# Banded attention between two feed-forward stages: rows transposed block by block, rotary products joined, work regrouped on four engines

## What is computed

```python
# hidden = layernorm(x); 16 heads of 64; b, s, _ = hidden.shape
q = rope(hidden @ Wq.T + bq)          # by head: x * cos + rot(x) * sin
k = rope(hidden @ Wk.T + bk)
v = hidden @ Wv.T + bv
# blocks of W = 128 positions; block n sees keys of blocks n - 1 and n
scores = einsum('bhnqd,bhnkd->bhnqk', qb, kcat) / sqrt(64)
band = (kj >= qi) & (kj <= qi + W)    # block 0 of a batch sees only its own keys
attn = softmax(where(valid, scores, -1e30))
ctx = einsum('bhnqk,bhnkd->bhnqd', attn, vcat)
x = x + merged(ctx) @ Wo.T + bo
```

## Time and profile before

| what | value |
|---|---|
| timed runs (3) | median 1627.08 us, 1626.82 to 1629.59 |
| the profiled execution's own time | 1629.63 us |
| its span, first to last instruction | 1627.8 us |
| TensorE busy, matrix products | 1503.2 us (92%) |
| VectorE busy | 1403.6 us (86%) |
| ScalarE busy | 1324.8 us (81%) |
| GpSimd busy | 1137.7 us (70%) |
| mean granted TensorE clock | 0.979 of full speed |

### The profile page before, as it was taken

One profiled execution on the slowest core, in us unless ns is written; L12 is line 12 of the kernel. 1 busy time (PEld: TensorE's weight loads), 2 busy tenths in 40 slices (PEclk: granted clock), 3 DMA queues, 4 the chain that ended last, 5 costly groups with the idle time before them and its releaser, 6 DMA issues. The chain is left out here.

```text
span 1627.8 us, 46830 instructions
## 1 busy us (share of the span) xinstructions
PE 1503.2 (92%) x16866; PEld 1145.2 (70%) x16866; DVE 1403.6 (86%) x3859; ACT 1324.8 (81%) x2442; POOL 1137.7 (70%) x911
## 2 busy tenths in 40 slices
PE   5999878899999999999999999999999999869998
PEld 4888745576767676666767676767676767658887
DVE  5999668899989999999999898999898889857885
ACT  5999658888878888888888787888788878749996
...
GB/s 210 92 124 99 65 100 128 169 164 176 169 183 159 176 161 184 165 187 170 170 184 157 172 166 169 168 176 172 173 151 175 165 166 159 172 157 69 109 111 70
DMA packets 728445, 247.92 MB, mean 152 GB/s; under 512 B 688148, under 2 KB 715032, under 8 KB 728216
## 3 DMA queue, kind: packets, MB, share of 16 engines
...
q10 hardware_dynamic: 704, 0.40, 0.1%
...
## 5 line engine op out<-in xcount | busy, mean ns | idle before, releaser
L1283 DVE CUSTOM_DVE_ANT_0 at_prob<-banks,at_masks,pre_s_scale 128x256 f32<-128x256 f32 (+1 forms) x1024 | 421.3, 472 | 25.8 <-PE banks L1697 9.3
L1446 ACT ACTIVATE at_prob<-at_prob,at_top 128x256 f32<-128x256 f32 (+1 forms) x1024 | 428.3, 490 | 16.5 <-DVE at_top L1283 14.1
L1295 DVE TENSOR_TENSOR at_halves<-at_prob,at_halves 128x1024 f16<-128x1024 f32 (+1 forms) x256 | 331.7, 1296 | 3.1 <-ACT at_halves L1455 3.1
L1582 PE MATMUL banks<-at_xt,pre_w_h 128*128 128x512 f16 x1024 | 299.4, 385 | 12.4 <-ACT at_v_l L1474 7.6
L1697 PE MATMUL banks<-at_kt,at_qt 32*128 32x256 f32 (+1 forms) x4096 | 253.4, 384 | 31.5 <-issue 20.8
L1455 ACT ACTIVATE at_halves<-at_prob 128x1024 f16<-128x1024 f32 (+1 forms) x256 | 263.4, 1029 | 6.1
L1697 PEld LDWEIGHTS banks<-at_kt,at_qt 32*128 32x128 f32 x4096 | 198.6, 187 | 93.1 <-issue 88.4
L1653 PE MATMUL banks<-at_v_h,at_pt 128*128 128x65 f16 x1984 | 208.9, 195 | 32.7 <-DMA at_pt<-at_halves 25.8
L1653 PEld LDWEIGHTS banks<-at_v_h,at_pt 128*128 128x128 f16 x1984 | 182.1, 98 | 73.2 <-DMA at_pt<-at_halves 41.0
L1175 POOL TENSOR_TENSOR at_kt<-at_k_by 128x512 f32<-128x512 f32 x128 | 171.5, 1340 | 77.3 <-DVE at_halves L1295 65.6
L1165 POOL TENSOR_TENSOR at_q_by<-at_q_first,at_tables 128x512 f32<-128x512 f32 x128 | 175.5, 1375 | 61.5 <-DVE at_halves L1295 60.8
...
## 6 DMA issues: line engine op xcount, KB each, us to landing
...
```

What stands on the lines that cost most here:

```text
L1283: last = nc.vector.tensor_tensor_reduce(out=prob[:, n % 2, h, low:2 * P], in0=s_ps[:, h, n % 2 * 2 * P + low:(n % 2 + 1) * 2 * P], in1=mas ...
L1295: nc.vector.tensor_tensor(parts[:, 1, :, :], prob[:, n % 2, :, keys_from(t, b):2 * P], parts[:, 0, :, :], ALU.subtract).then_inc(p_low, 1)
L1446: last = nc.scalar.activation(at, at, ACT.Exp, bias=top[:, n % 2, h:h + 1], scale=-1.0)
L1582: last = nc.tensor.matmul(pr_ps[:, half, :].rearrange("p (b t) -> p b t", b=SB), w[wp][:, k, at:at + P], xt[:, r, xp, :, k, :], start=n == ...
```

## The change

It has five parts, all in the attention stage.

- `x_halves` and `xt` are laid out by block, and `turn_x` transposes one block at a time, in SyncE's turn t block t + 7, behind the probabilities of block 2. Only the first group is still turned at once (`first_turn_x`). The load and the store of residual rows move behind it, and the load comes one turn earlier.
- The cosines and the sines of a group are loaded in different turns (`load_table`).
- GpSimd's turn has another order: the output bias comes first, the key rotation early, `context_low` last and for step t - 1 instead of t - 2, and the last query rotation waits for one more low half.
- VectorE makes its two products in one operation: the bank is read twice by a broadcast, the sine and cosine places are read as one piece (`key_products`, `query_products`), and the four semaphores of products become three.
- ScalarE's low half of the second pair of value blocks comes after two of the four exponentials of block 3 instead of after all four.

The core of the diff; the query's functions change as the key's do, and the indices of `x_halves` and `xt` where they are used follow the new layout:

```diff
-    x_halves = sb("x_halves", [P, 2, SB, C], F16)
-    xt = sb("xt", [P, 2, 2, SB, CK, P], F16)
+    x_halves = sb("x_halves", [P, SB, 2, C], F16)
+    xt = sb("xt", [P, 2, SB, 2, CK, P], F16)
...
-    k_made = [sem(f"k_product{n}") for n in range(4)]
-    q_made = [sem(f"q_product{n}") for n in range(4)]
+    k_first_made = [sem("k_first_by_cos"), sem("k_first_by_sin")]
+    q_first_made = [sem("q_first_by_cos"), sem("q_first_by_sin")]
+    k_second_made = sem("k_second_made")
+    q_second_made = sem("q_second_made")
...
+    def xt_turned(n):
+
+        S, blk = divmod(n, SB)
+        return 16 * (SB * (S // 2) + blk + 1) if S % 2 else 16 * (1 + SB * (S // 2 - 1) + blk + 1) if S else 16
+
     def xt_ready(S):
 
-        return 16 * (S // 2 + 1)
+        return xt_turned(SB * S + SB - 1)
...
-        def turn_x(S):
-
-            if big(S):
-                sp.wait_ge(x_low, SB * (S + 1))
+        def first_turn_x():
+            sp.wait_ge(x_low, SB)
+            sp.wait_ge(past.moved[0], past.stores(2 * past.SLOTS))
+            sp.dma_start(xt[:, 0, :, :, :, :].rearrange("p b e k t -> p (b e k) t"),
+                         x_halves[:, :, :, :].rearrange("p b e c -> p (b e c)"),
+                         transpose=True).then_inc(xt_in[0], 16)
+
+        def turn_x(n):
+
+            if step(n):
+                S, blk = divmod(n, SB)
+                sp.wait_ge(x_low, n + 1)
+                sp.wait_ge(xt_in[(n - 1) // SB % 2], xt_turned(n - 1))
                 need(v_done[1], NG * (S - 1))
-                if S < 2:
-                    sp.wait_ge(past.moved[S], past.stores(S + 2 * past.SLOTS))
-                sp.dma_start(xt[:, S % 2, :, :, :, :].rearrange("p e b k t -> p (e b k) t"),
-                             x_halves[:, :, :, :].rearrange("p e b c -> p (e b c)"),
+                if n == SB:
+                    sp.wait_ge(past.moved[1], past.stores(1 + 2 * past.SLOTS))
+                sp.dma_start(xt[:, S % 2, blk, :, :, :].rearrange("p e k t -> p (e k) t"),
+                             x_halves[:, blk, :, :].rearrange("p e c -> p (e c)"),
                              transpose=True).then_inc(xt_in[S % 2], 16)
...
-        def load_tables(S):
+        def load_table(S, e):
 
             if big(S):
-                for n in range(4):
-                    need(q_made[n], NG * (S - 1))
-                    need(k_made[n], NG * (S - 1))
+                for products in (*q_first_made, *k_first_made, q_second_made, k_second_made):
+                    need(products, NG * (S - 1))
                 at = SB * P * (S % SPB)
-                for e, table in enumerate((cos, sin)):
-                    sp.dma_start(tables[:, S % 2, e, :], table[:, at:at + SB * P]).then_inc(tab_in[S % 2], 16)
+                sp.dma_start(tables[:, S % 2, e, :], (cos, sin)[e][:, at:at + SB * P]).then_inc(tab_in[S % 2], 16)
...
             turn_p(t - 1, 3)
-            if g == 0:
-                turn_x(S + 1)
+            if t == -4:
+                first_turn_x()
             turn_context(t - 2)
             turn_p(t, 0)
-            load_residual(t - 4)
-            store(t - 6)
-            if g == 0 and S >= 0:
-                load_tables(S + 1)
             turn_p(t, 1)
             turn_p(t, 2)
+            if t + 7 >= SB:
+                turn_x(t + 7)
+            load_residual(t - 3)
+            store(t - 6)
             if t == -8:
                 load_x(SB)
             load_x(t + 13)
+            if g == 3 and S >= -1:
+                load_table(S + 2, 0)
+            if g == 1 and S >= 0:
+                load_table(S + 1, 1)
...
         def key(t, half):
 
             if step(t):
-                pool.wait_ge(k_made[2 * half], t + 1)
-                pool.wait_ge(k_made[2 * half + 1], t + 1)
+                pool.wait_ge(k_first_made[half], t + 1)
+                pool.wait_ge(k_second_made, t + 1)
                 need(s_done, 2 * t - 2)
                 need(k_carried, carried(t - 2))
                 nc.gpsimd.tensor_tensor(kt[:, half, own(t, 0):own(t, 0) + SB, :].rearrange("p s t -> p (s t)"),
-                                        k_by[:, 2 * half, :], k_by[:, 2 * half + 1, :],
+                                        k_by[:, half, :], k_by[:, 3 - half, :],
                                         (ALU.subtract, ALU.add)[half]).then_inc(k_roped[half], 1)
...
-            context_low(t - 2)
+            if t <= STEPS:
+                bias_rows(t - 5)
+            if t >= STEPS:
+                bias_rows(t - 4)
             key_product(t + 1, 0)
-            key_product(t + 1, 3)
+            key_product(t + 1, 1)
+            key(t + 1, 1)
             after_p_low(t, 0)
-            key(t + 1, 1)
+            key(t + 1, 0)
             query_product(t + 1, 0)
             after_p_low(t, 1)
-            query_product(t + 1, 3)
-            key(t + 1, 0)
+            query_product(t + 1, 1)
             query(t + 1, 1)
+            after_p_low(t, 2)
             query(t + 1, 0)
-            bias_rows(t - 4)
+            context_low(t - 1)
...
-        def key_product(t, n):
+        def key_products(t):
 
             if step(t):
                 r, g = t // NG % 2, t % NG
                 dve.wait_ge(tab_in[r], tab_ready(t // NG))
                 dve.wait_ge(k_done[1], t + 1)
-                need(k_roped[n // 2], t)
-                nc.vector.scalar_tensor_tensor(k_by[:, n, :], pr_ps[:, 1, :], bias[:, 1, 2 * g + 1:2 * g + 2],
-                                               tables[:, r, n % 2, :], ALU.add, ALU.mult).then_inc(k_made[n], 1)
...
-            query_product(t + 1, 2)
+            query_products(t + 1)
             context(t - 1, 1)
-            query_product(t + 1, 1)
             p_low_of(t, 0)
...
-            key_product(t + 2, 1)
-            key_product(t + 2, 2)
+            key_products(t + 2)
             p_low_of(t, 3)
...
-        def exponentials(t, b):
+        def exponentials(t, b, heads=range(GROUP)):
 
             if step(t):
                 n = 4 * t + b
                 act.wait_ge(top_made, n + 1)
-                for h in range(GROUP):
+                for h in heads:
                     at = prob[:, n % 2, h, keys_from(t, b):2 * P]
                     last = nc.scalar.activation(at, at, ACT.Exp, bias=top[:, n % 2, h:h + 1], scale=-1.0)
-                last.then_inc(p_made, 1)
+                if h == GROUP - 1:
+                    last.then_inc(p_made, 1)
...
-                need(xt_in[(S - 1) % 2], xt_ready(S - 1))
+                if S > 0:
+                    act.wait_ge(xt_in[(S - 1) % 2], xt_turned(n - SB))
...
-            exponentials(t, 3)
+            exponentials(t, 3, range(0, 2))
             v_low_of(t + 1, 1)
+            exponentials(t, 3, range(2, GROUP))
             v_low_of(t + 1, 0)
             p_high_of(t, 3)
...
-                    pe.wait_ge(q_made[1], t + 1)
-                    pe.wait_ge(q_made[2], t + 1)
+                    pe.wait_ge(q_second_made, t + 1)
...
```

57 lines of the change are left out of this document (32 added, 25 removed).

## The result

The changed kernel takes 1769.0 us, the median of four runs from 1766.68 to 1771.45; the kernel before took 1627.32 beside it (four runs, 1626.82 to 1629.59). The ratio is 1.0868, with a 95% interval from 1.0849 to 1.0887: 142 us slower, 8.7%. The forecast was 1722 in a range from 1655 to 1790.

The account below looks back on a forecast made before the run. TensorE, busy 92%, was taken as what counts, losing 0.45 us idle per quiet step and time in long periods at group starts. From 1627.1, minus 45 of gains, plus 140 for 14 standstills: 1722 us, range 1655 to 1790.

Parts of the forecast that it names:

- The wait that (5) adds: SyncE's queue: each group's first block transpose waits for the last values projection reading its buffer half; 14 standstills, 140 us.
- (5): SyncE's queue: transposing rows per block removes 3.28 us ahead of block 0's probabilities at group starts; gain 20 us (0 to 36).
- The size of a standstill: TensorE waiting for late probabilities: block 0 8.9 us late plus about 1 for the clock, together 10 us each.
- T0: End of the values projection on TensorE, 742.3 in the profile before; SyncE's delayed issues are counted from it.
- long periods: Two attention steps around every fourth step's start, 19.60 and 20.05 us against 18.44; some 42 us for 15 group starts.
- (1): VectorE's two rotary products as one operation: 1.18 us instead of 1.32, saving 0.28 us of VectorE per step.
- (2): ScalarE's value low halves amid block 3's exponentials: one copy, and the keys' projection with it, comes 0.85 us earlier.
- (4): SyncE's table loads spread over turns: the issue cost is hidden by a pause in every step, so no gain.
- (3): GpSimd's new order: last query rotation ends at 956.7 instead of 957.4; with (1) and (2) TensorE gains 25 us.
- Rival A: Standstill half covered, block 3's probabilities landing in 3.0 us: 6.5 us each, gains 55, 1663 us; chance 0.15.
- rival C: No standstill, SyncE's wait being met before it comes to it; only the gains count, 1582 us; chance 0.07.
- B: Knock-on: late block 0 delays block 2 and the next block 3; 15 us per standstill, gains 25, 1812 us; chance 0.10.

Follow-up runs that it names:

- late_turn: The changed kernel with each row transpose one turn later (block t + 6 in turn t instead of t + 7): 1624.01 us, ratio 0.9962.
- kept_busy: The changed kernel with 64 extra unused TensorE products at the start of its turn in each of the 14 standstill steps: 1770.42 us, ratio 1.0874.
- turn_alone: The kernel before with only the new layout and the block-wise row transposes at the change's place (block t + 7): 1734.56 us, ratio 1.0646.
- turn_last: The changed kernel with the row transpose moved to the end of SyncE's turn, behind residual load and store, row load and table: 1725.31 us, ratio 1.0616.
- late_oldpool: The late_turn kernel with GpSimd's turn in the order of the kernel before: 1606.1 us, ratio 0.9855.

## Why the prediction was right

By its steps. The sum was 1627 - 45 + 140 = 1722; measured, in its own terms, it is 1627 - 6 + 148 = 1769, with the gains from late_turn's ratio (10.4 to 10.6 us per standstill, by times or by ratios).

**The wait that (5) adds: right.** Fourteen waits of SyncE for the values projection, at every fourth step, 11.8 us each (forecast 10 to 13). The count argument gave place and number, and late_turn shows that one turn's shift takes away all of it.

**The size of a standstill: right, 10.4 us for 10, with one part otherwise.** The issue began at T0 + 3.5 in the row above, forecast 3.9; block 3's products at T0 + 8.6, forecast 8.5. Then the prediction had block 0 0.35 us late and 1 us for the clock. Block 0's wait didn't come. TensorE took 6.6 us from block 3's first product to block 0's (965.00 to 971.63), where the earlier trace rows have 4.35, so 2.3 us went at a fallen clock (0.50, then 0.76); that hid block 0's landing. Together 8.6 + 2.3 = 10.9 in this one, 10.4 on average. kept_busy shows that the two are not to be added: where the clock stayed up, block 0's wait came in its place. The standstill cost only 8.9 us in turn_alone, where fewer transfers are queued behind the wait; turn_last shows the same from the other side.

**(5), the gain of the moved transposes: right.** 16 us for 20. The 42 us of long periods that it was taken from was too high, though: by the earlier trace rows all 63 periods together are only 1189 - 63 x 18.44 = 27 us longer than quiet ones.

**(1) joined products: the operation was right, 1.20 us for 1.18**, and by itself worth some 7 us (0.42%). **(2) low halves: nothing.** **(4) tables: nothing, as forecast.**

**(3) GpSimd regrouped: this is the step that failed.** It said that the last query rotation ends at 956.7 instead of 957.4 and that the scores gain. In its place TensorE waits for `at_qt` no less with the new order than with the old one, 28.8 us in late_turn and this in late_oldpool:

```profile
PE banks L1719 <- POOL at_qt L1204: 22.0, 20, 1.7
```

Its waits for VectorE's tops are 9.9 us for 2.7, and the order costs 18 us beside the other parts and 51 alone. The prediction counted GpSimd's operations as if their times stayed the same in any place, and the last rotation as half of a pair of 3.48 us. The two are not alike (GpSimd, then VectorE, kernel before):

```profile
953.92 2.25 POOL L1185 TENSOR_TENSOR at_qt<-at_q_by 128x512 f32<-128x512 f32 x1
```

```profile
956.13 1.26 POOL L1185 TENSOR_TENSOR at_qt<-at_q_by 128x512 f32<-128x512 f32 x1
```

```profile
953.69 1.34 DVE L1295 TENSOR_TENSOR at_halves<-at_prob,at_halves 128x1024 f16<-128x1024 f32 x1
```

The first is held up by block 2's low half, which ends at 955.03, and ends itself at 956.17; the last one takes 1.26 and can't start earlier than that. A new wait for an event at 955.0 doesn't bring it forward to 956.7. The price of an operation depended on what the other engine did, and the reordering changed just that. The 0.45 us of idle ahead of the scores may itself come from this held-up pair; no run shows it.

So of the 45 us of gains some 6 came. Of the 39 missing, some 18 are the price of GpSimd's order (late_turn against late_oldpool), and 4 are (5). The other 17 are TensorE's 0.45 us of idle per step, which the prediction let (1) to (3) remove for 25 us: with the old order all the parts together gain 24 us, 16 of them from (5), so 8 are left for these. The gains were thus the term mis-sized, 39 of the 47 us between 1722 and 1769; the standstills make the other 8. What holds a quiet step at 18.3 us stays open. The quiet steps "near 18.0" were named as what would show it, with 25 us more if they stayed at 18.4; they went to 18.97 in the median. Sign and mechanism of the loss were right, the gains were not: the time came out inside the range because the standstills are nearly four times as large as the error in the gains. Rival A (1663) and rival C (1582) fell, since the landing took 4.8 to 5.3 us and not 3.0, and the wait was there; B's 15 us per standstill was not reached.
